# A fused adaLN transformer layer: a hand-written order of units, single transposes, and split products for one more pair of heads

## What is computed

```python
def _L0_attn_ref(x, Wq, Wkv, Wo, bo):
    ...
    q = (x @ Wq).reshape(b, n, HEADS, DIM_HEAD).transpose(0, 2, 1, 3)
    kv = (x @ Wkv).reshape(b, n, 2 * KV_HEADS, DIM_HEAD)
    k = kv[:, :, :KV_HEADS].transpose(0, 2, 1, 3)
    v = kv[:, :, KV_HEADS:].transpose(0, 2, 1, 3)
    ...
    q = q * cos + _rotate_half(q) * sin
    k = k * cos + _rotate_half(k) * sin
    k = jnp.repeat(k, g, axis=1)
    v = jnp.repeat(v, g, axis=1)
    dots = jnp.einsum('bhid,bhjd->bhij', q, k) * SCALE
    attn = jax.nn.softmax(dots, axis=-1)
    out = jnp.einsum('bhij,bhjd->bhid', attn, v)
    out = out.transpose(0, 2, 1, 3).reshape(b, n, HEADS * DIM_HEAD)
    return out @ Wo + bo
...
mod = (_silu(L0_c) @ L0_wmod).reshape(L0_c.shape[0], 6, 1, -1)
sa, ca, ga, sb, cb, gb = (mod[:, 0], mod[:, 1], mod[:, 2], mod[:, 3], mod[:, 4], mod[:, 5])
...
h = _layernorm(x, axis=-1) * (1 + ca) + sa
x = x + ga * _L0_attn_ref(h, L0_attn_Wq, L0_attn_Wkv, L0_attn_Wo, L0_attn_bo)
h = _layernorm(x, axis=-1) * (1 + cb) + sb
x = x + gb * _L0_ffn_ref(h, L0_ffn_w1, L0_ffn_b1, L0_ffn_w2, L0_ffn_b2)
return x
```

## Time and profile before

| | us |
|---|---|
| Median of 3 runs | 736.14 |
| Lowest and highest run | 735.33, 736.24 |
| Profiled execution, its own time | 736.22 |
| Profiled execution, span from the first to the last instruction | 734.4 |
| TensorE busy in the span | 680.9 (93%) |
| ScalarE, VectorE, GpSimd busy in the span | 552.7 (75%), 530.4 (72%), 430.8 (59%) |
| Chain that ended last: TensorE, "issue", VectorE, GpSimd, ScalarE | 52%, 17%, 16%, 9%, 4% |

### The profile page before, as it was taken

One profiled execution on the slowest core, in us unless ns is written; L12 is line 12 of the kernel. 1 busy time (PEld: TensorE's weight loads), 2 busy tenths in 40 slices (PEclk: granted clock), 3 DMA queues, 4 the chain that ended last, 5 costly groups with the idle time before them and its releaser, 6 DMA issues.

```text
span 734.4 us, 13498 instructions
## 1 busy us (share of the span) xinstructions
PE 680.9 (93%) x3733; PEld 520.1 (71%) x3733; DVE 530.4 (72%) x1195; ACT 552.7 (75%) x1148; POOL 430.8 (59%) x397
## 2 busy tenths in 40 slices
...
DMA packets 31580, 24.75 MB, mean 34 GB/s; under 512 B 16688, under 2 KB 26944, under 8 KB 31552
## 3 DMA queue, kind: packets, MB, share of 16 engines
...
...
## 4 chain that ended last, share of the span: by engine, by line
PE 52%; issue 17%; DVE 16%; POOL 9%; ACT 4%; DMA 1%; DVEq 1%; SPq 0%; ACTq 0%; POOLq 0%
PE unit_ps L926 8%; PE o_ps L972 7%; DVE o_t L733 5%; PE o_ps L961 4%; PE score_ps L944 4%; PE score_ps L946 4%; PE unit_ps L910 4%; PE unit_ps L899 4%; PE o_ps L1027 4%; POOL probs_lo L485 4%; POOL rot_sum L471 3%; PE unit_ps L883 2%; DVE rot_b L720 2%; PE unit_ps L884 2%; PE unit_ps L885 2%
## 5 line engine op out<-in xcount | busy, mean ns | idle before, releaser
L485 POOL TENSOR_TENSOR probs_lo<-probs,probs_hi 128x512 fp32r<-128x512 f32 x160 | 202.4, 1282 | 51.4 <-ACT probs_hi L621 51.4
L471 POOL TENSOR_TENSOR rot_sum<-rot_a,rot_b 128x512 f32<-128x512 f32 (+1 forms) x96 | 106.2, 1106 | 161.4 <-DVE rot_b L720 161.1
L728 DVE TENSOR_REDUCE w_all<-unit_ps 128x2 f32<-128x512 f32 x256 | 166.4, 684 | 13.9 <-PE unit_ps L910 12.8
L618 ACT ACTIVATE probs<-score_ps 128x512 f32<-128x512 f32 x256 | 147.3, 589 | 4.2 <-PE score_ps L946 0.8
L910 PEld LDWEIGHTS unit_ps<-k_hi,q_hilo 128*128 128x128 f32 x512 | 92.2, 191 | 51.0 <-issue 14.3
L475 POOL TENSOR_TENSOR qk_rot<-rot_sum,qk_rot 128x512 fp32r<-128x512 f32 (+1 forms) x96 | 105.3, 1103 | 26.7 <-ACT qk_rot L570 26.7
L910 PE MATMUL unit_ps<-k_hi,q_hilo 128*128 128x256 f32 x512 | 112.2, 303 | 5.3 <-DVE o_t L733 4.4
L899 PEld LDWEIGHTS unit_ps<-ident_r,qk_rot 128*128 128x128 f32 x640 | 93.2, 193 | 30.8 <-issue 16.1
L733 DVE TENSOR_TENSOR o_t<-o_un,unit_ps 64x256 f32<-64x256 f32 x248 | 103.6, 418 | 13.8 <-PE unit_ps L920 9.6
L944 PE MATMUL score_ps<-q_hilo,k_hi 128*128 128x512 f32 x256 | 108.8, 425 | 1.5 <-DMA q_him<-neg_max_t 1.5
L899 PE MATMUL unit_ps<-ident_r,qk_rot 128*128 128x128 f32 x640 | 101.4, 285 | 1.7 <-POOL qk_rot L475 1.5
...
## 6 DMA issues: line engine op xcount, KB each, us to landing
...
q_him<-neg_max_t SPq DMA_DIRECT2D x64, 4.0 KB
...
sums<-o_un SPq DMA_DIRECT2D x32, 8.0 KB, 2.0
```

The costliest lines, as they stand in the source:

```text
L471: pool.tensor_tensor(total, rot_a[k % 2][:, 0:heads, :], rot_b[k % 2][:, 0:heads, :], ALU.add).then_inc(rot_summed, 1)
L485: pool.tensor_tensor(probs_lo[s % 2][:, jc, :, :], probs[s % 2][:, jc, :, :], probs_hi[s % 2][:, jc, :, :].bitcast(F32), ALU.subtract).the ...
L618: ins = act.activation(probs[s % 2][:, jc, :, :].rearrange("p h i -> p (h i)"), score_ps[jc][:, :], ACT.Exp, scale=SCALE)
L728: dve.tensor_reduce(neg_max[u[1] // 4][:, first:first + C], ps[:, :].rearrange("p (c j) -> p c j", c=C), AX.X, ALU.max, negate=True).then_ ...
```

## The change

The table `UNITS` and the pattern `WORK` are replaced by `SLOTS`: eight lines, one for each slot, in which each word is one piece of work. S0 and S1 are the halves of the scores; "m" is the next of six parts of the product with v (a plain pair does its two fp32 products at the first and the fourth); a word such as qt5 or xT0 is one transpose of 128 columns, so the unit qt5 is done when the fourth of its words has been passed; all other units are one word. stats, rstd, norm and recip now stand in the same lines. TensorE follows the words one by one; the other engines see a unit at the place of its last word. The order of the units, and with it the turn of the four banks, is the new one.

```diff
-UNITS = [
-    [("s", 4), ("s", 5), ("s", 6), ("s", 7), ("xT", 0), ("qt", 4), ("mT", 1)],
-    [("qkv", 0, 2), ("s", 8), ("qkv", 1, 2), ("qt", 5), ("s", 9)],
...
+SLOTS = [
+    "S0 s4 s5 m s6 m s7 xT0 xT0 m m S1 m qt4 qt4 m mT1 qt4 qt4",
+    "S0 m s8 S1 m qkv02 qt5 qt5 qt5 qt5 qkv12 m m m m",
...
-STATISTICS_AT, NORMALISE_AT, RECIPROCALS_AT = 4, 6, (5, 2)
...
-SPLIT_PAIRS = (1, 3, 4, 5, 7)
-
-
-WORK = [("un",), ("scores", 0), ("scores", 1), ("pv", 0), ("pv", 1), ("pv", 2), ("pv", 3)]
+SPLIT_PAIRS = (0, 1, 3, 4, 5, 7)
...
 def slot_order(st, s):
 
-    held = {"scores": st.attn, "pv": st.attn if s >= 1 else st.out, "un": st.attn if s >= 2 else st.out}
-    rest, order = units(st, s), []
-    for w in WORK:
-        if held[w[0]]:
-            order.append((None, w))
-            if rest and w[0] in ("scores", "pv"):
-                order.append(rest.pop(0))
-    return order + rest
+    return [(PLACE[w[1]], w[1]) if w[0] == "part" else (None, w)
+            for w in slot_parts(st, s) if w[0] != "part" or w[3]]
...
-            def unit(st, place, u):
+            def unit(st, place, u, part, last):
...
-                    for h in range(2):
-                        for ch in range(C):
-                            ins = pe.matmul(ps[:, h * N + ch * P:h * N + (ch + 1) * P],
-                                            qk_rot[:, ch, first + h, :, :].rearrange("p t d -> p (t d)"),
-                                            ident_r[:, :], start=True, stop=True)
+                    h, ch = part // 2, part % 2
+                    ins = pe.matmul(ps[:, part * P:(part + 1) * P],
+                                    qk_rot[:, ch, first + h, :, :].rearrange("p t d -> p (t d)"),
+                                    ident_r[:, :], start=True, stop=True)
...
-                p, v, chunks = [(probs_hi, v_hi, (0, 1)), (probs_hi, v_lo, (0, 1)),
-                                (probs_lo, v_hi, (0,)), (probs_lo, v_hi, (1,))][part]
-                for jc in chunks:
-                    ins = pe.matmul(o_ps[i][0:DH + 1, :], v[par][:, jc, g, :], p[i][:, jc, :, :].rearrange("p h i -> p (h i)"),
-                                    start=part == 0 and jc == 0, stop=part == 3)
-                if part == 3:
+                p, v = [(probs_hi, v_hi), (probs_hi, v_lo), (probs_lo, v_hi)][part // 2]
+                jc = part % 2
+                ins = pe.matmul(o_ps[i][0:DH + 1, :], v[par][:, jc, g, :], p[i][:, jc, :, :].rearrange("p h i -> p (h i)"),
+                                start=part == 0, stop=part == 5)
+                if part == 5:
                     ins.then_inc(pv_done, 1)
```

More of the change, by code:

```diff
@@ L48, with parsed @@
 EPS = 1e-5
-UNITS = [
[8 rows of a table removed]
-]
-ALL_UNITS = [(slot, u) for slot, units in enumerate(UNITS) for u in units]
+SLOTS = [
[8 rows of a table added]
+]
+def parsed(slots):
+    every, n, found = " ".join(slots).split(), 0, []
+    for text in slots:
+        slot, product = [("un",)], 0
+        for word in text.split():
+            kind = word.rstrip("0123456789")
+            number = word[len(kind):]
+            if kind == "S":
+                slot.append(("scores", int(number)))
+            elif kind == "m":
+                slot.append(("pv", product))
+                product += 1
+            elif kind in ("stats", "rstd", "norm", "recip"):
+                slot.append((kind, int(number or 0)))
+            else:
+                name = (kind, *map(int, number)) if kind == "qkv" else (kind, int(number))
+                slot.append(("part", name, every[:n].count(word), word not in every[n + 1:]))
+            n += 1
+        found.append(slot)
+    return found
+ORDER = parsed(SLOTS)
+ALL_UNITS = [(slot, w[1]) for slot, order in enumerate(ORDER) for w in order if w[0] == "part" and w[3]]
+PARTS = {w[1][0]: w[2] + 1 for order in ORDER for w in order if w[0] == "part" and w[3]}
+PLACE = {u: k for k, (_, u) in enumerate(ALL_UNITS)}
 LATE_UNITS = ([("qt", s) for s in range(4, PAIRS)] + [("s", h) for h in range(4, HEADS)] + [("mT", q) for q in range(1, 4)]
@@ L177, in units, with slot_parts @@
             if has(st, u) and (TAIL_AT[u] if st.tail else s) == slot]
[L180 to L189 removed]
+def slot_parts(st, s):
+    if st.tail and s > 1:
+        parts = [("part", u, part, part == PARTS[u[0]] - 1) for _, u in units(st, s) for part in range(PARTS[u[0]])]
+        return [("recip", 1)] * (s == TAIL_RECIPROCALS_AT) + parts
+    held = {"scores": st.attn, "pv": st.attn if s >= 1 else st.out, "un": st.attn if s >= 2 else st.out,
+            "stats": st.norm, "rstd": st.norm, "norm": st.norm}
+    return [w for w in ORDER[s]
+            if (not st.tail and has(st, w[1]) if w[0] == "part" else not st.tail and (st.attn, st.out)[w[1]] if w[0] == "recip"
+                else held[w[0]])]
+def slot_order(st, s):
+    return [(PLACE[w[1]], w[1]) if w[0] == "part" else (None, w)
+            for w in slot_parts(st, s) if w[0] != "part" or w[3]]
 def rotated(st, s, end):
@@ L816, in step @@
                             unit(st, place, w)
+                        elif w[0] == "stats":
+                            if st.number == -1:
+                                dve.wait_ge(x_in, 48)
+                            statistics(st.count(1, 1, 2), 0 if st.number == B - 2 else st.batch(2))
+                        elif w[0] == "norm":
+                            normalise_tokens(st.count(1, 1, 2), 0 if st.number == B - 2 else st.batch(2))
+                        elif w[0] == "recip":
+                            reciprocals(st, w[1], -w[1])
                     if st.number == -1 and s == SIGNS_AT:
@@ L928, in unit @@
                 if kind == "zT":
-                    pe.wait_ge(z_ready, st.count(1, 1, -1))
-                    for ch in range(C):
-                        ins = pe.transpose(ps[:, ch * P:(ch + 1) * P], z_sb[:, ch * P:(ch + 1) * P], ident[:, :])
-                ins.then_inc(unit_full, 1)
+                    if part == 0:
+                        pe.wait_ge(z_ready, st.count(1, 1, -1))
+                    ins = pe.transpose(ps[:, part * P:(part + 1) * P], z_sb[:, part * P:(part + 1) * P], ident[:, :])
+                if last:
+                    ins.then_inc(unit_full, 1)
             def scores(st, s, jc):
```

46 lines of the change are left out of this document (18 added, 28 removed), and 12 rows, old and new, of tables (SLOTS, UNITS).

## The result

The changed kernel takes 716.23 us (median of 4 runs, 715.82 to 716.82) beside 736.19 for the kernel before in the same session: a ratio of 0.973, 95% interval 0.9713 to 0.9747, so 20 us faster. The forecast was 708.7 in a range of 690 to 727, 7.5 us too low. The profiled execution's span is 714.0 beside 734.4.

What follows compares the result with a forecast made beforehand. TensorE was taken as the bound, with 2.65 us of waits a step. -0.31 - 0.36 - 1.2 = -1.87 us in 14 full steps (-26.2), plus 1.3 saved in steps 0 and 15: 736.2 - 27.5 = 708.7 us, range 690 to 727.

Steps and rivals of the forecast that it cites:

- the edges: Steps 0 and 15 gain 1.3 us together from split and single transposes; no change ahead of step 0 or behind step 15.
- The order: Reordered units in each full step remove TensorE's old waits but bring new ones: net -1.2 us a step.
- new waits: Five TensorE waits expected in the new order, at s8, s6 (with mT1), mT3, kt1 and mT2: 1.45 us a step.
- old ones: Five TensorE waits in the old step, at qkv(0,2), s14, yT0, mT2 and s0, with unhidden loads: 2.65 us.
- s8: s8 waits for ScalarE's copy of qt4, queued behind exponentials and mT1: 0.3 us plus 0.1 for the load, 0.4.
- mT3: mT3 waits for s15 behind VectorE's queue: 0.15 us with the semaphore plus 0.1 for the load, 0.25.
- s6: s6 waits for the bank of bc3: 0.15 us plus 0.1 load; with under 0.1 at mT1, 0.35.
- mT2: mT2 waits for s11 behind reciprocals and two maxima: taken as 0.3 us, between about 0.1 and 0.75.
- The walk: Stepping through the new order with profiled operation times to find waits; it found five, 1.45 us a step.
- The lone transposes: Nine more transpose runs a step, each making one transpose cost 0.06 instead of 0.11 us: some -0.36 a step.
- The split: Pair 0 as six fp32r products instead of two fp32 ones: about -0.31 us in each of 16 steps.
- The conversion: VectorE's cast in the reciprocals ahead of mT2; if long beside GpSimd, 0.75 instead of 0.3 us: 6.3 more, hence 715.

Runs made afterwards that it cites:

- order alone: Changed kernel with pair 0 as a plain pair and each unit's transposes in runs of four, leaving only the new unit order: 717.85 us, ratio 0.9746.
- pair 0 plain: Changed kernel with pair 0 back to two fp32 products and two exponentials, new order and single transposes kept: 712.26 us, ratio 0.9674.

## Why the prediction was right, and where it was not

The direction was right and the time lies in the range; the gain is 20.0 us of the 27.5 forecast. The full steps give 1.66 us each where the forecast had 1.87 (2.9 us over 14), and the edges cost 2.9 where it had a gain of 1.3 (4.2 us): together the 7.1 by which the span misses. Some of the agreement in the parts is luck.

**The order** was the right reason, and the largest. Alone it gives 39.64 - 38.08 = 1.56 a step. The forecast's net of 1.2 set 1.45 of new waits against 2.65 of old ones. In the changed kernel's step the new ones are: s8 0.49 (forecast 0.4), mT3 0.29 (0.25), kt1 0.13 (0.15), s6 0.1 (0.35 with mT1), mT2 none (0.3), and two that I hadn't seen: s4 0.24, for ScalarE's copy of qt3, and pair 0's first product 0.17. Sum 1.42. That it comes so near the forecast's 1.45 is luck: three places were hit within 0.1, two priced too high by 0.55 together, and two missed that are worth 0.41. The walk lost where it looked at the unit and not at the product ahead of it: pair 0's first product needs the same ScalarE queue as s8.

**The lone transposes** seem to be sized right, 0.36 a step between order alone and pair 0 plain, but that too is luck. They start as expected:

```profile
299.12 0.22 PE L926 MATMUL unit_ps<-ident_r,qk_rot 128*128 128x128 f32 x1
299.18 0.40 PE L999 MATMUL o_ps<-probs_lo,v_hi 128*65 128x512 f32 x1
299.41 0.22 PE L926 MATMUL unit_ps<-ident_r,qk_rot 128*128 128x128 f32 x1
299.47 0.45 PE L972 MATMUL score_ps<-q_hilo,k_hi 128*128 128x512 f32 x1
299.75 0.40 PE L974 MATMUL score_ps<-q_him,k_lo 65*128 65x512 f32 x1
```

Each takes 0.06, and the product behind it 0.23 (299.18 to 299.41) where its weights have 65 columns and 0.28 (299.47 to 299.75) where they have 128. So ahead of 128-column weights a lone one costs 0.06 + 0.05, as much as a member of a run, and the gain comes only ahead of the others, which the forecast didn't ask. Slots 5 and 6, which hold six of the additional runs, gain 0.11: from yT0 to pair 5's first product it is 9.25 in order alone (292.29 to 301.54) and 9.14 in pair 0 plain (290.06 to 299.20). Slot 0 gains 0.27 (4.60 and 4.33 from S0 to S0), but 0.2 of it is the wait at mT1 that the runs bring about, and 0.06 the transposes. So the lone transposes themselves are worth some 0.17 a step, half of the forecast, and the rest was cover for mT1, which the sum hadn't asked for. With pair 0 split, s8's wait swallows what slot 0 gains, and 2.1 us of the 5.6 are left. With these sizes the rows add up: 2.65 - 1.42 of waits, 0.31 of the split's products and 0.17 make 1.71 of the 1.75 (39.78 - 38.03) by which the step is shorter.

The rule of the Trainium skill (page "TensorE: Matmul & The Clock Gate", section "Part 3: Packing small matmuls"), that loads hide only where row groups differ, would have left no gain in slots 5 and 6. The 0.11 there, and 0.06 for a lone transpose beside 0.11 in a run, speak against it here.

**The split** is the step that failed. Its 0.31 of products is real, as the sum of the rows, and I set the two exponentials against a whole step's room on ScalarE and one wait of 0.4. The runs showed a loss of 0.26 a step and 4.0 us in all in the new order, and no gain in the old one. The sum put 0.31 on the path without asking where in the step it falls: it saves 0.62 ahead of s8, where ScalarE sets the time, and costs 0.31 behind it, where TensorE does. Of the 0.26 the exponentials alone make 0.12, with long products over the wait of s8; the rest comes with the short products, which leave that wait open.

**The conversion** was the place to look at: at mT2 it is short in the changed kernel and mT2 waits for nothing, and moving qkv(0,2) made it long, with a wait of 0.78, about the 0.75 that the forecast had priced. The rule cited for it (the Trainium skill, page "SBUF — State Buffer", section "Who interferes with whom") agrees with the four rows of that experiment: the cast, and the subtraction with two operands in SBUF, end with a GpSimd operation, while the maxima, whose kind the page says never contends, keep their length (1.27 for two there, 1.29 in the changed kernel, where GpSimd idles).

**The edges** I set at a gain of 1.3 in steps 0 and 15 and at no change ahead of them and behind, and together they cost 2.9. Step 15 is 1.3 longer. In it there are no kt transposes between the maximum of s15 and mT3:

```profile
629.21 0.63 PE L999 MATMUL o_ps<-probs_lo,v_hi 128*65 128x512 f32 x2
630.80 0.30 PE L941 MATMUL unit_ps<-ident,w_all 128*128 128x128 f32 x1 [0.96 <-DVE w_all L758]
```

That is 1.1, and the edit that moves mT3 won back 0.96. A unit that covers a wait in a full step has to be looked for in the partial steps too. Of the prologue's 1.0, 0.64 lies ahead of the signs (30.77, before 30.13), whose start goes up to 31.47 with the same step -1; that part stays open. The other 0.4 is gone in pair 0 plain, which takes 11.80 from there to S0 (31.16 to 42.96), beside 12.22 and, before, 11.84; its granted clock from 36 to 43 is 0.98, in the changed kernel 0.50, so this part goes with the clock. The MLP's code is the same in all kernels, and its stretch goes from 69.0 to 71.0, so the 0.8 there is not shown to come from the change.
